# Two reorderings in a four-layer convolution kernel: small offset products three products later, and an eviction by halves

## The reference, cut to what matters

```python
x = x + L0(gn(x))   # 3x3 offset conv to 3 channels; bilinear sample at the offsets; depthwise 3x3; pointwise
x = x + L1(gn(x))   # 3x3 mean pool; 3x3 offset conv to 27 channels; deformable 3x3 conv 128 -> 128
x = x + L2(gn(x))   # plain 3x3 conv 128 -> 128 with rebuilt weights
x = x + L3(gn(x))   # 1x1 projections, strip attention along rows and columns, gates, 1x1 projection
```

## Time and profile before

| | |
|---|---|
| time before, median of 3 runs | 1719.94 us (1717.85 to 1722.87) |
| the profiled execution's own time | 1719.42 us |
| its span | 1717.6 us |
| PE busy, matmul records | 1591.8 us (93% of the span), 7252 |
| DVE busy | 1141.4 us (66%) |
| ACT busy | 659.3 us (38%) |
| mean granted clock of TensorE | 0.958 |

### The profile page before, as it was taken

How to read it: one execution, slowest core, us unless ns; L and a number is a source line. 1 busy time by engine, 2 the same in 40 slices (tenths; PEclk the granted TensorE clock), 3 DMA queues, 4 the chain that set the end, 5 groups by cost and what they waited for, 6 DMA issues and landing times.

```text
span 1717.6 us, 22494 instructions
## 1 busy us (share of the span) xinstructions
PE 1591.8 (93%) x7252; PEld 837.6 (49%) x7252; DVE 1141.4 (66%) x2139; ACT 659.3 (38%) x1066; POOL 50.2 (3%) x76
## 2 busy tenths in 40 slices
PE   2979999999999999999999999999999999999975
PEld 1537453565435554365534645355543655337422
DVE  4358349864598457883498835985469844887266
ACT  2126224461345413453244622555134541346131
POOL 2000000000000000000000000000000000000000
PEclk8989999999999999999999999999999999999987
DMA  3000000100001000000001000010000100000000
GB/s 117 14 13 2 7 1 1 51 5 4 1 1 52 7 2 1 26 27 7 1 1 51 2 6 1 1 52 7 2 1 14 39 7 2 1 25 2 1 0 25
DMA packets 7971, 24.61 MB, mean 14 GB/s; under 512 B 1664, under 2 KB 2368, under 8 KB 7792
## 3 DMA queue, kind: packets, MB, share of 16 engines
q1 hardware_dynamic: 7792, 22.40, 3.5%
HBM read 12.13 MB, written 8.39 MB: 12 GB/s over the span
## 4 chain that ended last, share of the span: by engine, by line
PE 75%; DVE 11%; issue 6%; ACT 4%; SPq 3%; DMA 1%; POOL 1%; DVEq 0%; POOLq 0%; ACTq 0%
PE psN L516 14%; PE psO L516 13%; PE psN L851 11%; PE psO L720 7%; PE psN L720 5%; PE psN L627 4%; PE psO L576 4%; SPq L414 3%; ACT samp L932 2%; DVE samp L1662 2%; PE psN L594 2%; PE psN L558 2%; PE psN L564 2%; PE psM L500 2%; PE psN L901 1%
## 5 line engine op out<-in xcount | busy, mean ns | idle before, releaser
L516 PE MATMUL psO<-samp,w 128*128 128x512 f32 x576 | 285.2, 631 | 0.0
L516 PE MATMUL psN<-xn,w 128*128 128x512 f32 x576 | 278.7, 605 | 1.7 <-DVE yout L1409 0.9
L1143 ACT ACTIVATE samp<-psN,vec 128x512 f32<-128x512 f32 x160 | 110.0, 687 | 130.4 <-PE psN L851 130.4
L516 PEld LDWEIGHTS psO<-samp,w 128*128 128x128 f32 x576 | 106.6, 200 | 102.6 <-issue 96.2
L1317 DVE COPY xblk<-psN 120x256 f32<-120x256 f32 x128 | 54.3, 424 | 142.7 <-PE psN L558 142.7
L932 ACT ACTIVATE samp<-psN 128x576 f32<-128x576 f32 x192 | 118.2, 676 | 58.1 <-PE psN L627 58.0
L516 PEld LDWEIGHTS psN<-xn,w 128*128 128x128 f32 x576 | 98.3, 189 | 84.5 <-issue 84.5
L932 ACT ACTIVATE G<-psN 120x256 f32<-120x256 f32 x128 | 49.1, 383 | 229.6 <-PE psN L564 229.6
L720 PE MATMUL psN<-img,w 128*128 128x512 f32 x288 | 133.4, 608 | 0.0
L720 PE MATMUL psO<-img,w 128*128 128x512 f32 x288 | 133.0, 603 | 0.0
L627 PE MATMUL psN<-GQt,xq 64*128 64x144 f32 x1536 | 123.1, 297 | 10.6 <-ACT samp L932 9.0
(11 more groups left out here) (156 smaller groups left out, 2299.9 us busy)
## 6 DMA issues: line engine op xcount, KB each, us to landing
xin<-in_x SPq DMA_DIRECT2D x16, 512.0 KB, 4.1
out<-yout SPq DMA_DIRECT2D x16, 512.0 KB, 3.7
pool_v<-rows SPq DMA_DIRECT2D x72, 25.5 KB
w<-in_w SPq DMA_DIRECT2D x2, 576.0 KB, 5.1
samp<-in_r SPq DMA_DIRECT2D x1, 576.0 KB, 6.8
tab<-in_tab SPq DMA_DIRECT2D x1, 513.0 KB, 5.3
kh_w<-in_kh SPq DMA_DIRECT2D x1, 320.0 KB, 5.4
kv_w<-in_kv SPq DMA_DIRECT2D x1, 320.0 KB, 5.6
```

Of the source, the lines that this page charges most:

```text
L516: last = mm(dst[:, h, :], wgt[:, k, :], rhs(h, k), start=(k == 0), stop=(k == K9 - 1))
L1143: nc.scalar.activation(out, bank(m)[0:out.shape[0]], fn, **kw).then_inc(l3_act.sem, 1)
```

## The change

Three things are done. `next_offsets` goes from hook (1, 3) to (1, 6), and `start_far` from (1, 6) to (1, 8). VectorE's seven steps of `start_hat` for the first image go from ahead of the layer-1 residual to behind its statistics. `offset_parts` signals after each half, `parts` copies each half when it is there and signals for it, and `offsets` takes the even tiles first and waits for the second half ahead of tile 1.

```diff
-        parts_product = signal("parts_product", 2)
+        parts_product = signal("parts_product", 4)
-        parts_ready = signal("parts_ready", 3)
+        parts_ready = signal("parts_ready", 5)
@@ offset_parts
-                last.then_inc(parts_product.sem, 1)
+                    last.then_inc(parts_product.sem, 1)
@@ offsets
-                pe.wait_ge(parts_ready.sem, parts_ready.at(i, max(n, 1)))
-                for t in range(TILES):
+                for t in (0, 2, 4, 6, 1, 3, 5, 7):
+                    if t < 2:
+                        pe.wait_ge(parts_ready.sem, parts_ready.at(i, (1, 2 * n - 2 + t)[n > 0]))
@@ one_pass, TensorE
-                            hooks[1, 3] = next_offsets
-                            hooks[1, 6] = lambda: start_far(i + 1)
+                            hooks[1, 6] = next_offsets
+                            hooks[1, 8] = lambda: start_far(i + 1)
@@ parts, ScalarE
-                act.wait_ge(parts_product.sem, parts_product.at(i, n - 1))
                 for b in range(2):
-                    last = copy(off_parts[s]...[:, :, b], psO[s][:, b, :]...)
-                last.then_inc(parts_ready.sem, 1)
+                    act.wait_ge(parts_product.sem, parts_product.at(i, 2 * n - 3 + b))
+                    copy(off_parts[s]...[:, :, b], psO[s][:, b, :]...).then_inc(parts_ready.sem, 1)
@@ one_pass, VectorE
                         start_flag(own, i + 1)
-                        for part in range(START_HAT):
-                            start_hat(own, i + 1, 0, part)
                     dve.wait_ge(conv_ready.sem, conv_ready.at(i, 3 + s))
...
                     stats(own, ("L2A", "L2B")[s], order)
+                    if s and more:
+                        for part in range(START_HAT):
+                            start_hat(own, i + 1, 0, part)
                     affine(own, ("L2A", "L2B")[s], order)
```

More of the change, by code:

```diff
@@ L973, in parts @@
                 s = n % 2
-                act.wait_ge(parts_product.sem, parts_product.at(i, n - 1))
                 for b in range(2):
-                    last = copy(off_parts[s].rearrange("p (j b r c) -> p j b r c", b=2, j=STRIPS, c=SW)[:, :, b],
-                                psO[s][:, b, :].rearrange("p (r j c) -> p j r c", j=STRIPS, c=SW))
-                last.then_inc(parts_ready.sem, 1)
+                    act.wait_ge(parts_product.sem, parts_product.at(i, 2 * n - 3 + b))
+                    copy(off_parts[s].rearrange("p (j b r c) -> p j b r c", b=2, j=STRIPS, c=SW)[:, :, b],
+                         psO[s][:, b, :].rearrange("p (r j c) -> p j r c", j=STRIPS, c=SW)).then_inc(parts_ready.sem, 1)
             def tap_rows(j):
```

## The result

The changed kernel takes 1681.12 us (median of 4 runs, 1679.39 to 1682.67) against 1719.64 for the kernel before (4 runs, 1717.85 to 1722.87). The ratio is 0.9774 with a 95% interval of 0.9756 to 0.9791: 38.5 us faster, where 1682.5 us and 36.9 us faster were forecast. The profiled execution took 1681.28 us with a span of 1679.3. Lines of the changed kernel count one or two higher than before (L500 is L502, L516 is L518, L564 is L566, L602 is L604, L1528 is L1529, L1419 is L1420).

A forecast was written before the change was run, and what follows sets the result against it. TensorE, busy 93% of the span, bounds the kernel through idle time and half clock. Gains 35.8 + 1.1 + 0 = 36.9 us, from 1719.42 to 1682.5 us; forecast range 1679 to 1688 (0.68), 8 in 10 for 1677 to 1694.

The forecast's parts named there:

- Wait and clock: Small offset products moved three products later: TensorE's 2.16 us wait and the half clock behind it go, gain 35.8 us.
- rival A: Clock still falls at the moved small products, 2.0 us a pass, 14 us in all: 1696 us; chance 0.12.
- Hats: VectorE's seven steps behind the residual's statistics: cost and gain 0, first product's slack 1.0 us where it was 3.2.
- Halves: Copies by halves at the pass start: gain only in passes 0 and 1, 0.8 and 0.35 us, together 1.1 us.
- Doubles: `doubles` at the pass start, 1.81 us at half clock, 1.01 at full: no change, bounds -2.4 and +4.7 us.
- B: VectorE's queue delays the first block's product; a us late costs 3 us a pass; no gain 0.04, slower 0.03.
- C: Halves pay in full ahead of L1528 in passes 2 to 6: 4 to 5 us more, 1678 us; chance 0.07.
- D: Copies come after TensorE in most passes, some wait ahead of the small products stays: 1686 to 1700 us; chance 0.04.

The follow-up runs named there:

- e5: Kernel before with two useless products ahead of the small offset products at their old hook (1, 3): 1704.9 us, ratio 0.992.
- e6: Changed kernel with the small offset products at hook (1, 5) instead of (1, 6): 1684.1 us, ratio 0.9796.
- e1: Kernel before with only the two hooks moved, hats still ahead of the residual, evictions whole: 1697.3 us, ratio 0.990.
- e9: Changed kernel with two useless products between the small products and `doubles` at the start of each pass: 1677.0 us, ratio 0.9764.
- e12: Kernel before with hooks and hats moved, evictions whole, one useless product on either side of a pass's first small products: 1678.2 us, ratio 0.9766.
- e3: Kernel before with the evictions by halves and the tile order alone: 1711.7 us, ratio 0.9969.
- e7: Changed kernel with three useless VectorE operations (2.1 us in all) between the hats and the affine form: 1697.3 us, ratio 0.9872.
- e10: Changed kernel with three one-element VectorE operations in its idle time ahead of the layer-1 residual: 1692.4 us.
- e11: Changed kernel with six one-element VectorE operations in its idle time ahead of the layer-1 residual: 1680.8 us.

## Why the prediction was right

**Wait and clock.** The step from the trace held: the wait of 2.16 us and the half clock behind it went in seven of seven passes. It was forecast at 35.8 us and measured at 32.1. The path behind it is 4.87 us long and not 4.60: 1.88 for the small products where I took 1.75, 1.91 and 0.97 for the three products around the flag where I took 1.72 and 0.86, so these three cost 0.3 us more than I had taken. And TensorE came 0.7 us behind the copies, where I had 0.4. That is 0.5 us in each of seven passes. The argument, that the clock holds through small products if nothing is idle around them, held in all seven passes; e5 and e6 show how near the edge is. The sentence of the Trainium skill (TensorE: Matmul & The Clock Gate, "Part 4: PE-mode transpose") didn't decide here; no run of this case has transposes alone. The price that rival A put on a fall, 2.0 us at least, is 1.7 in e5 and e6.

**Hats.** Forecast 0, measured 2.2 us: the residual, some 0.8 us late before, had cost TensorE 0.04 to 0.57 us in each pass (C to F 10.16 to 10.69, then 10.12), behind the group mean, at the first product of `layer0`. I had priced only what the move delays, not what it lets come sooner. The slack of the first product was forecast as 1.0 us and is 0.6: I had counted to the product and not to its weight load. The text didn't say what the move is for; e1 does: without it, 14 us of the gain are given back.

**Halves.** Forecast 1.1 us. With the clock of `doubles` held equal they are worth 1.2 us by the medians of e9 and e12 and 0.3 by the ratios. The step itself held: in pass 1 the time from `store_ready` to L1528 fell from 1.03 to 0.71 us (0.35 forecast), in pass 0 L1528 came 1.3 us sooner in e3 (0.8 forecast; the profiles scatter by 1 to 2 us here, with a mean of 117.1 over six kernels with whole evictions and 115.9 over eight with halves), in the passes 2 to 6 nothing moved. The count by TensorE alone would have given 8 us or more. It was the chain, with issue ahead of L1528 and not L500, that kept it out, against the list of waits, which names L500.

**Doubles.** Forecast 0, measured 1.9 us in the profile (long in three passes, where five had been). The bounds of -2.4 and 4.7 are a little wide; from the eight lengths they come to -2.1 and 4.3. The ground for the 0, idle time of the same sum in one piece and not two, is the weak step: by the comparison behind e12 the one piece is probably the better one.

So the sum came out by errors that cancel: 3.7 us too much for the first edit, 2.2 too little for the hats, 1.9 for the clock of `doubles`, and 0.6 to 1 that I can't place. The point, 1682.5, is 1.4 us off; that it is so near is in part luck.

**The rivals.** A: the clock fell in none of seven passes; e6 shows that it is a rival of weight if 0.9 us of the cover is gone. B: the mechanism exists at the place and from the point named (e7), but a us late costs 1.3 us (1.4 for the 1.12 of e7), not 3; the clock did not fall behind the idle stretch of 1 us there in any pass. C: out as a mechanism, though the halves' whole gain (5.4 us in e3) comes near its price. D: not seen; TensorE came 0.6 to 0.7 us behind the copies in each pass.

## What to carry to other kernels

A wait of TensorE beside very small products costs more than its length: here 2.2 us of wait brought 1.7 to 3.3 us of half clock (S to C of 9.05 and 10.67 us before, 7.35 in e5), and covering it fully, with something to spare, paid more than twice the wait. Before a wait is counted as gain, follow the chain to the engine that takes the result: where that engine comes late by itself, the list of waits names the wrong one. When a wait goes, whatever lay in its shadow (here 3.2 us of hats) has to be moved in the same change.

## What the hardware showed that was not expected

The turn of VectorE's loop, with the same instructions behind and ahead of it, took 0.6 to 1.0 us in most kernels, and 1.7 to 2.0 us in two, e7 and e10, with three more operations in the loop's body; with six more it took 0.7 to 0.9 (e11). Over the six turns this was 6 to 7 us, and e10, where nothing else waits for the added operations, was 11 us slower in all, the clock of `doubles` behind the later turn included. And idle time alone did not bring TensorE's clock down: 1.4 us of it ahead of a group mean (e1) and 1.0 us ahead of L566 (e7), both between full products but for two or four short records, did nothing in any pass, 0.2 us ahead of 16 small products (e5, e6) went with a fall in two passes of seven, and the same small products without idle time (the 63 passes above) with none. Why the two cases differ, the runs don't show.
